# A fused four-layer kernel: the weight quantising of the feed-forward spread over more slots of the attention loop, its loads issued one batch later, and one scale worked out sooner

## The reference, cut to what matters

```python
# layer 0, attention: 16 heads of 64, softmax over 375 context positions
x = x + tanh(g_xattn[0]) * xattn(layernorm(x), ctx, Wq, Wk, Wv, Wo, bo)
# layer 0, feed-forward with quantised weights and activations
def lpbq_dequant(w):                      # blocks of 32 inputs, 4 bits
    wb = w.reshape(O, I // 32, 32)
    s = max(max|wb| over the block / 7, 1e-12)
    return clip(round(wb / s), -8, 7) * s
def act_qdq(x):                           # one scale for the whole tensor
    scale = max(max|x| / 32767, 1e-12)
    return clip(round(x / scale), -32768, 32767) * scale
x    = act_qdq(layernorm(x))
up   = act_qdq(x @ lpbq_dequant(w_up).T)
gate = act_qdq(x @ lpbq_dequant(w_gate).T)
sig  = fixed_qdq_u16(sigmoid(gate))
gate = act_qdq(gate * sig)
o    = act_qdq(gate * up)
out  = o @ lpbq_dequant(w_down).T         # x = x + tanh(g_ffn[0]) * out
```

## Time and profile before

| | |
|---|---|
| Median of 3 runs | 1616.03 us (1612.99 to 1617.35) |
| The profiled execution | 1614.3 us, of which the span from first to last instruction is 1612.4 us |
| Granted TensorE clock, mean | 0.943 of full speed |
| Attention layer 0 | from the start to about 660 us; its 16 batches of 8 slots start at 32 us |
| Feed-forward layer 0 | about 660 to 846 us |
| TensorE, VectorE, ScalarE busy | 1407.1, 1227.9, 1109.4 us |

### The profile page before, as it was taken

The page is one execution under the profiler, slowest core; times in us unless marked ns, Lnnn a source line. Parts: engine busy times, 40 slices in busy tenths (PEclk is TensorE's granted clock), DMA queues, the critical chain, the costliest instruction groups (busy, mean ns, idle before and its releaser), DMA issues. The chain is left out here.

```text
span 1612.4 us, 40506 instructions
## 1 busy us (share of the span) xinstructions
PE 1407.1 (87%) x15436; PEld 993.6 (62%) x15436; DVE 1227.9 (76%) x3143; ACT 1109.4 (69%) x2448; POOL 160.5 (10%) x171
## 2 busy tenths in 40 slices
PE   5899997999999999692478989889898699999996
PEld 3566675667666666440456666666666367788884
DVE  5888886888888888468778999898898877344443
ACT  4777775777777776477328888888888554366663
POOL 1000000000000000000000000000000100034443
PEclk8999999999999999796689999999999789999998
DMA  6223314232223221000011212110100162122221
GB/s 191 75 93 96 95 38 144 86 95 86 86 88 106 88 77 34 1 0 27 0 57 51 86 45 83 49 61 19 32 22 11 34 241 68 56 35 48 48 45 24
DMA packets 65229, 105.68 MB, mean 66 GB/s; under 512 B 7497, under 2 KB 39474, under 8 KB 63890
## 3 DMA queue, kind: packets, MB, share of 16 engines
q1 hardware_dynamic: 58322, 94.83, 18.8%
q0 software_dynamic: 6720, 8.27, 3.1%
HBM read 68.88 MB, written 35.11 MB: 64 GB/s over the span
## 5 line engine op out<-in xcount | busy, mean ns | idle before, releaser
L1396 ACT ACTIVATE a_p<-a_s,a_nb 112x375 f32<-112x375 f32 x256 | 141.2, 600 | 26.5 <-DVE a_nb L1498 26.3
L105 PE MATMUL a_ps_o<-a_vh,a_pt 125*128 125x64 f16 (+1 forms) x1536 | 152.7, 183 | 2.6 <-ACT a_pt L1409 0.8
L1316 PE MATMUL a_ps_t<-ident,a_p 112*128 112x112 f32 x768 | 117.3, 282 | 42.9 <-ACT a_p L1396 41.7
L523 ACT ACTIVATE a_p<-a_ps_s,a_nb 112x375 f32<-112x375 f32 x256 | 144.4, 573 | 13.6 <-DVE a_scaled L683 12.9
L107 PE MATMUL a_ps_o<-a_vh,a_pt 125*128 125x64 f16 (+1 forms) x1536 | 151.1, 182 | 0.0
L106 PE MATMUL a_ps_o<-a_vl,a_pt 125*128 125x64 f16 (+1 forms) x1536 | 151.0, 182 | 0.0
L105 PEld LDWEIGHTS a_ps_o<-a_vh,a_pt 125*128 125x128 f16 x1536 | 133.4, 97 | 14.9 <-ACT a_pt L1409 6.6
L1316 PEld LDWEIGHTS a_ps_t<-ident,a_p 112*128 112x128 f32 x768 | 78.9, 144 | 97.9 <-issue 82.4
L106 PEld LDWEIGHTS a_ps_o<-a_vl,a_pt 125*128 125x128 f16 x1536 | 130.7, 98 | 11.0
L531 ACT ACTIVATE a_pt<-a_ps_t 125x336 f16<-125x336 f32 x256 | 101.5, 448 | 48.7 <-PE a_ps_t L455 48.1
L1498 DVE CUSTOM_DVE_ANT_0 a_s<-a_s,a_fill 112x375 f32<-112x375 f32 x256 | 130.3, 547 | 5.5
(11 more groups left out here) (447 smaller groups left out, 4483.2 us busy)
## 6 DMA issues: line engine op xcount, KB each, us to landing
a_piece<-in_w SPq DMA_DIRECT2D x72, 256.0 KB, 3.1
split_weights<-a_pair SPq DMA_DIRECT2D x72, 256.0 KB, 3.3
w<-split_weights SPq DMA_DIRECT2D x8, 1024.0 KB, 6.3
a_ctx<-in_ctxT SPq DMA_DIRECT2D x16, 375.0 KB, 3.8
ctx<-a_cx SPq DMA_DIRECT2D x16, 375.0 KB, 5.1
a_cx<-ctx SPq DMA_DIRECT2D x16, 375.0 KB, 5.9
w1h<-split_weights SPq DMA_DIRECT2D x2, 1792.0 KB, 14.3
w1l<-split_weights SPq DMA_DIRECT2D x2, 1792.0 KB, 16.2
```

Source lines behind the costliest of these rows:

```text
L105: nc.tensor.matmul(out, wh, mh, start=(i == 0), stop=False)
L523: nc.scalar.activation(p32[:, g % 2, i, 0:NC], ps_s[0:S, i, 0:NC], ACT.Exp, bias=nb[:, g % 2, i:i + 1], scale=SC, accum_out=rsum[:, h:h + ...
L1316: mm = nc.tensor.matmul(ps_t[:, 2 * (g % 2) + i, t * S:(t + 1) * S], p32[:, g % 2, i, t * KV:t * KV + 128], ident32[0:S, 0:S], start=(t == ...
L1396: nc.scalar.activation(p32[:, g % 2, i, 0:NC], s2[:, g % 2, i, :], ACT.Exp, bias=nb[:, g % 2, i:i + 1], scale=-1.0).then_inc(exp_done, 1)
```

## The change

Three tables and three places of code change. `QUANT_AT` moves the halves from batches 2, 3, 5, 6, 7, 10 to 2, 4, 6, 8, 10, 12. The steps move from slot 3 to slot 6 of that batch, the values from slot 6 to slot 2 of the next one. The load of half i is issued in round `QUANT_AT[i]` of SyncE's loop instead of the round before. `T_AT` moves the transposes accordingly. The statistics of a row block move from slot 5 to slot 0 of the batch after (with a table for the last few). In the feed-forward, `gated_product` is cut in two, and the scale of the up product is worked out after the first part of number 4 and not after the whole of it.

```diff
-        QUANT_AT = {0: 2, 1: 3, 2: 5, 3: 6, 4: 7, 5: 10}
-        T_AT = {(3, 3): ("T0", 0), (3, 6): ("T1", 0), (4, 3): ("T0", 1), (4, 6): ("T1", 1), (6, 3): ("T0", 2),
...
+        QUANT_AT = {0: 2, 1: 4, 2: 6, 3: 8, 4: 10, 5: 12}
+        T_AT = {(3, 3): ("T0", 0), (3, 6): ("T1", 0), (6, 3): ("T0", 1), (6, 6): ("T1", 1), (7, 3): ("T0", 2),
+                (7, 6): ("T1", 2), (10, 3): ("T0", 3), (10, 6): ("T1", 3), (11, 3): ("T0", 4), (11, 6): ("T1", 4),
+                (12, 3): ("T2", 4), (13, 3): ("T0", 5), (13, 6): ("T1", 5), (14, 3): ("T2", 5)}
+        STATISTICS_AT = {NP * (b + 2): b for b in range(B - TG - 1)}
+        STATISTICS_AT.update({NP * 12 + 5: 11, NP * 14: 12, NP * 15: 13, NP * 15 + 5: 14})
...
-                    if b == QUANT_AT[i] - 1:
+                    if b == QUANT_AT[i]:
                         load_quant(i)
...
-                if 1 <= b and p == 5:
-                    dve.wait_ge(job_lo, NUMBER["W", b - 1] + 1)
-                    nc.vector.bn_stats(row_stats[:, b - 1, :], x_res[:, b - 1, :]).then_inc(row_done, 1)
+                if g in STATISTICS_AT:
+                    t = STATISTICS_AT[g]
+                    dve.wait_ge(job_lo, NUMBER["W", t] + 1)
+                    nc.vector.bn_stats(row_stats[:, t, :], x_res[:, t, :]).then_inc(row_done, 1)
                 for i in QUANT_AT:
-                    if b == QUANT_AT[i] and p in (2, 3, 6):
-                        {2: block_scales, 3: block_steps, 6: block_values}[p](i)
+                    if g == NP * QUANT_AT[i] + 2:
+                        block_scales(i)
+                    if g == NP * QUANT_AT[i] + 6:
+                        block_steps(i)
+                    if g == NP * QUANT_AT[i] + 10:
+                        block_values(i)
...
             def gated_product(o):
+                round_sigmoid(o)
+                multiply_gate(o)
...
-            gated_product(4)
+            round_sigmoid(4)
             dve.wait_ge(mx_all, 2)
             scale_of(am[:, UP:UP + 1], sc[:, 0:1], sc[:, 4:5], sc[:, 1:2]).then_inc(scal, 1)
+            multiply_gate(4)
             gated_product(5)
```

More of the change, by code:

```diff
@@ L198, in attention0_phase @@
         FLAT_ROW_AT = {NP * b + p + i: TG * n + i for n, (b, p) in enumerate(((13, 4), (14, 3), (15, 1))) for i in range(TG)}
-        QUANT_AT = {0: 2, 1: 3, 2: 5, 3: 6, 4: 7, 5: 10}
-        T_AT = {(3, 3): ("T0", 0), (3, 6): ("T1", 0), (4, 3): ("T0", 1), (4, 6): ("T1", 1), (6, 3): ("T0", 2),
-                (6, 6): ("T1", 2), (7, 3): ("T0", 3), (7, 6): ("T1", 3), (8, 3): ("T0", 4), (8, 6): ("T1", 4),
-                (10, 3): ("T2", 4), (11, 3): ("T0", 5), (11, 6): ("T1", 5), (12, 3): ("T2", 5)}
+        QUANT_AT = {0: 2, 1: 4, 2: 6, 3: 8, 4: 10, 5: 12}
[4 more added lines that the diff above has]
+        STATISTICS_AT.update({NP * 12 + 5: 11, NP * 14: 12, NP * 15: 13, NP * 15 + 5: 14})
         JOBS = [[("V00", 0), ("V01", 0)], [("V02", 0), ("K7", 0), ("K0", 1)], [("OT1", -1), ("Q0", 1), ("K1", 1)],
@@ L1010, in gated_product, with round_sigmoid @@
             def gated_product(o):
+                round_sigmoid(o)
+                multiply_gate(o)
+            def round_sigmoid(o):
                 dve.wait_ge(sig_raw, o + 1)
@@ L1013, in gated_product, with multiply_gate @@
                                         ).then_inc(sig_rounded, 1)
+            def multiply_gate(o):
                 dve.wait_ge(sig_rounded, o + 1)
```

## The result

| | before | after |
|---|---|---|
| Median of the runs taken together, 4 each | 1614.55 us (1612.99 to 1617.35) | 1595.78 us (1594.64 to 1599.54) |
| Ratio | 1 | 0.989 (95% interval 0.9875 to 0.9905) |
| The profiled execution: time, span | 1614.3, 1612.4 us | 1599.54, 1597.6 us |

The change makes the kernel about 18 us faster: the ratio says 17.8 us (1.1% of 1614.55; 15.3 to 20.2 by its interval), the two medians lie 18.8 us apart. The forecast was 1600.4 us with a range from 1596.5; the median lies 0.7 us under that range. The profiled execution of after was the slowest of its four, so its span alone understates the gain. A second set of 4 runs gave 1594.58 us and a ratio of 0.9883 (0.9867 to 0.99).

What follows compares the result with a forecast made beforehand. TensorE was taken to bound the attention loop, the chain of whole-tensor scales the feed-forward. Terms 9.9 + 2.7 + 0 + 3.0 = 15.6 us, taken from the median 1616.03, gave 1600.4 us, range 1596.5 to 1607.

Steps and rivals of the forecast that it cites:

- Part 1: Attention loop, batch 5: loads one batch later remove SyncE's 29.8 us wait and TensorE's stall, 9.9 us gained.
- the transfer's own stall: Rival: the w_down transfer itself starves the pieces, the stall moves to a later batch, only 5.7 us gained; 5 in 100.
- the loads come too late: Rival: VectorE waits in slot 2 for late halves, up to 9.6 us each, 1658 us in all; 2 in 100.
- the other reading: Batch 5: the low TensorE clock has another cause and stays, so the later loads give 8.0 us, not 9.9.
- Part 2: Attention loop: spreading scales, steps and values over slots closes five gaps before the scores of slot 5, 2.7 us gained.
- no named gap behind them: Slot 6 of the loop: steps moved there, where values stood, at the same length, open no gap; no loss counted.
- up to 1.4 us: Batches 13 and 14: loss if values (0.95 us) and about 0.45 of a T job come through; 0.2 taken.
- The new wait of T0: Attention loop: T0 now stands one slot behind the values, but they end 1.5 us early; price 0.
- Part 3: Attention loop: statistics moved to slot 0 cost 0; slot 5 gains at most 0.7 us in batches 13 and 14.
- cover for the statistics: Slot 0, before the maxima of slot 1: 0.8 us slack against 0.33 net, price 0; 4.3 us if absent.
- Part 4: Feed-forward: the up scale worked out sooner starts ScalarE 3.7 us sooner and gains 3.0 us, bounds 2.0 to 3.3.
- nothing back: Rival, feed-forward: the GpSimd wait eats the move or the gated scale was the bound; 12.6 us gained, 1603.4; 4 in 100.

Runs made afterwards that it cites:

- e1_loads: Kernel before with only the loads of the halves issued one round later, old tables kept: 1605.24 us, ratio 0.9946.
- e4_spread: Changed kernel's tables for quantising and transposes, with loads one round early, statistics and feed-forward as in the kernel before: 1602.04 us, ratio 0.9936.
- e5_stats_back: Changed kernel with the statistics of the row blocks put back into slot 5: 1595.87 us in one run.
- e2_stats: Kernel before with only the statistics moved from slot 5 to slot 0 of the next batch: 1611.23 us, ratio 0.9979.
- e6_source: Kernel before with the load of half 4 reading w_up instead of w_down, queue and waits kept: 1612.5 us in one run.
- e9_tables: Changed kernel with halves in batches 1, 3, 5, 7, 9, 11, layer-norm rows in other slots, two blocks' statistics moved again: 1596.34 us, ratio 0.9887.
- e8_pieces: Changed kernel with the split of one expert piece moved from slot 4 to slot 2: 1598.28 us in one run.
- e11_order: Changed kernel with ScalarE's exponentials of slot 5 ahead of the high half of that slot's first job: 1615.03 us in one run.
- e7_port: Changed kernel with the up scale one step sooner still, ahead of the rounding of gated block 4: 1596.49 us in one run.

## Why the prediction came out as it did

| Part | predicted | measured | from |
|---|---|---|---|
| 1, loads later | 9.9 | 9.5 | e1_loads, L and M |
| 2, spread slots | 2.7 | 2.9 | e4_spread against e1_loads, L and M |
| 3, statistics | 0 | 2.4 (3.0 on the kernel before, 0.5 of it in the stalled batch) | e5_stats_back, e2_stats |
| 4, up scale | 3.0 | 3.1 | F |
| Sum | 15.6 | 17.7 | L, M and F of before and after |

The parts add up to 17.9 us, so they hardly touch one another. The experiments cut parts 1 and 2 at another place than the prediction did: it had put batch 5's own gap into part 1, and e1_loads left that gap standing. With its 0.67 us moved over, part 1 measures 10.2 and part 2 2.2 us.

**Part 1 was right, in place and in size.** The stall was SyncE's queue standing behind one wait. e6_source, with other data and the same wait, kept it whole; so the rival "the transfer's own stall" is out, and so is "the loads come too late", as no wait of VectorE for a half appeared. That the lower clock was a consequence and went too is read from the 1.00 in the stretch of batch 5, which took 37.72 us and not 47.84. Both 9.5 and 10.2 lie nearer to 9.9 than to the 8.0 of the other reading. The Trainium skill, in "TensorE: Matmul & The Clock Gate" (What's actually happening), calls the low clock the default that activity releases, and the trace agrees: 0.51 behind the stall, 1.00 where there is none. One thing I had not said: the spread alone would have been enough (e4_spread).

**Part 2 was right in place and 0.5 us too high.** All five gaps of slot 5 went, and batch 5's too (slot 4 of every batch from 2 to 12 is 4.47 or 4.48 us). The statement that the steps have "no named gap behind them" in slot 6 fails in batches 4 and 8, where a layer-norm row stands beside them. There slot 7 takes 5.01 us and not 4.72; the weight load waits:

```profile
218.18 0.10 PEld L105 LDWEIGHTS a_ps_j<-a_cx,a_wk 128*128 128x128 f16 x1 [0.50 <-DVE a_kl L658]
```

That is 0.6 us lost in both together, and the gaps that went were each a little larger than the 0.6 us of their bracket (5.15 to 4.47). For batches 13 and 14 I had feared up to 1.4 us; these two batches grew by 0.85 us in e5_stats_back, nearly all of it by the T jobs that left earlier batches; the gap before the scores of slot (13,5) grew from 0.35 to 0.51 us, and slot (14,4) gave 0.08 back. The new wait of T0 cost nothing, as priced.

**Part 3 is the step that failed.** I argued that slot 0 has cover for the statistics, which held: no gap came before the scores of slot 2, though e9_tables showed that the cover does not hold a layer-norm row as well. And I argued that slot 5 gains nothing outside batches 13 and 14, because no gap was named behind its statistics. That rested on the waits of the matmuls alone. The 0.33 us net went through the maxima and the low half to the weight load of the Q job, in each batch from 1 to 11 (0.27 us, or 0.17 where slot 6 holds a T or X job) and in batch 14 (0.33), not in batch 13: 2.4 us, where the prediction had 0 and a bound of 0.7. That is the whole miss in the stretches, 17.7 against 15.6, and a little more.

**Part 4 was right.** VectorE waited 0.24 us for the spread (I took 0.3) and 1.85 us for the first gated block (I took 1.8), and F fell by 3.07. The rival "nothing back" is out, and the gated scale is now what ends last: ScalarE waits 0.60 us for it in after (the row at 736.82), near the 0.65 us between the prediction's 753.9 and 754.55.

**The rest of the miss** is the starting value. I took the 15.6 us off the median of three runs, 1616.03. With a fourth it is 1614.55. From there the sum gives 1598.95; the 2.1 us of the stretches make it 1596.85, and what is left to 1595.78 is 1.1 us, within the spread of the unchanged parts (below). Where the two medians fell in their scatter is chance; the 2.1 us are not.

What stays open: whether another order could win the 0.31 us gap without what e11_order paid for it. Only these two ways, e8_pieces and e11_order, were tried.

## What to carry to other kernels

When you ask whether an instruction on another engine is covered, read the waits of the weight loads as well as those of the matmuls: a wait of 0.48 us stood there in every batch from 1 to 12, and no matmul showed a gap for it. One semaphore wait at the head of a transfer queue holds back all that is queued behind it; ask for each such wait how old the awaited work will be, since one batch more made 29.8 us into none. And judge a small gain by the length of its stretch, since the whole time carries the scatter of everything else.

## What the runs showed of the hardware

- The spread over the partitions took 1.12 us beside VectorE's conversion to uint16 and 0.35 us beside an idle VectorE (e7_port), 3.2 times as long.
- Parts with identical instructions differ between runs by more than the parts of this change are worth. Attention layer 1, nearly whole, in before, in after and in the second set of after:

```profile
835.00:1270.00 435.00, 388.20 (x5092) 264.28 (x5093) 389.27 (x1124) 374.24 (x680) 11.92 (x16) 0.95 0.14 43
```

```profile
816.00:1254.00 438.00, 392.25 (x5088) 268.74 (x5088) 388.44 (x1123) 373.54 (x679) 11.86 (x16) 0.93 0.14 43
```

```profile
818.00:1250.00 432.00, 386.35 (x5088) 263.85 (x5089) 387.45 (x1123) 372.45 (x678) 11.91 (x16) 0.95 0.14 43
```

From its first scores to its last it took 433.1, 437.7 and 431.5 us, and the granted clock was 0.95, 0.93 and 0.95. VectorE and ScalarE did the same work in all three (within 2 us), TensorE was busy 4 to 6 us longer at the lower clock. What set the clock lower in one of them no run here shows.
- The second slot of the whole loop took 4.47 us in some runs and 5.8 to 6.0 in others of the same code. The granted clock separates them: 0.70 in this slot of before, 1.00 in this slot of the second set of after, with TensorE's work the same:

```profile
35.95:41.72 5.77, 5.66 (x24) 3.09 (x24) 2.15 (x7) 2.55 (x8) 0.00 (x0) 0.70 0.00 0
```

```profile
36.77:41.25 4.48, 3.98 (x26) 2.35 (x26) 2.16 (x7) 2.56 (x8) 0.00 (x0) 1.00 0.00 0
```

In both TensorE had been idle for 1.86 us before the slot's first scores. Why the clock fell behind it in one and not in the other no run here shows.
